# Expert matmuls over 512-column chunks that run across expert borders, in a one-core adaLN block

## The chip, the cores and the metric

The kernel runs on one core of one Trainium2 chip. The metric is the device time of one execution in microseconds. Of the kernel before there are three timed runs and one profiled execution.

## The reference

One block on 4096 tokens of 256 channels, everything in fp32. A state-space mixer (layer norm, projection to 768, a causal convolution, a 16-state scan over the tokens, gating, projection back) is followed by a mixture of 16 experts around one attention. Only the latter's projections are touched:

```python
w = jax.nn.softmax(masked, axis=-1)                # n x 16 expert weights

def moe_proj(p):                                   # p: 16 x 256 x 128
    y = jnp.einsum('nc,ech->neh', x, p)
    return jnp.einsum('ne,neh->nh', w, y)
q = moe_proj(q_proj).reshape(b, t, -1)
k = moe_proj(k_proj).reshape(b, t, -1)
v = moe_proj(v_proj).reshape(b, t, -1)
```

Each token's q, k and v are sums over all 16 experts of the expert's projection times the token's weight for it. Then come softmax attention and an output projection, again summed over experts.

## The kernel before

The tokens are cut into NB = 8 blocks of BT = 512, and each block into TT = 4 tiles of P = 128. The kernel has three parts: preparation of the first block, eight slots with the expert projections (one per block), and attention with the output projection.

A slot has STEPS = 64 steps, one for each tile t and expert e (s = 16 t + e). At a step TensorE multiplies the tile's 128 tokens (256 channels, KC = 2 halves) with the expert's q, k and v weights side by side, H3 = 384 columns (L1470 to L1478). For precision each fp32 operand is split into a high and a low part, and three products are summed: six matmuls per step, all into one PSUM bank. Four banks (MOE_BANKS) are used in turn, and TensorE waits on `moe_acc` until the accumulate of four steps ago is done. VectorE then adds the bank's 384 columns, times the token's weight, onto `acc`: one instruction per step (L1244 for the first expert of a tile, L1247 otherwise), each waiting for `moe_mm` and for the accumulate before it.

`acc` is a part of the tensor `wst`; the high and low weights lie in `w_hi` and `w_lo`, with the layout [P, KC, E, 3, H], so that the experts of one half of the channels are contiguous.

Between the steps both engines run pieces of the work on the following blocks, at step numbers that are written out by hand. Names and steps (later by three in the first slot):
- The scan of the next block has nine links: at steps 1, 3, 5 ... 17 TensorE issues a few small matmuls (`scan_piece`, L1356, L1357, L1359) and VectorE adds their result (`scan_step`, L969). Each link waits for the add before it.
- VectorE's norm pieces of the block after next stand at steps 2, 6, 9, 12 and 15: statistics (L892, L897), modulation (L908), shift (L915), statistics again, normalisation (L902). If a step has both, the norm piece stands before the scan add.
- At step 24 TensorE computes y (L1369), at 27 the output projection of the mixer (L1379), and VectorE adds the residual at 29 (`x2_piece` 0, L996). From step 31 on, six projections (`project`, L1323) follow at one per step; the first waits for that addition. VectorE has convolution pieces (L949) at steps 35 and 39.
- The transposes of the second norm's result stand at step 40 (L1389), the router's logits (L1397) at 44, the input of the scan (L1334) at 49, and VectorE's routing pieces (L1027 to L1090) at 46 to 56.
- At e = 4 of a tile TensorE transposes q and k of the tile before (L1404, L1405), and at e = 6 VectorE takes their low parts (L1119).

Slots 0 to 5 have all of this. Slot 6 has no norms, convolutions or projections, since there is no block after next. Slot 7 has only score maxima for the attention (`max_piece`).

Of the kernel before, what the change touches and what calls it, by code (L numbers as in the profile page):

```python
# [7 lines left out]
ALU = mybir.AluOpType  # L8
# [4 lines left out]
def adaln_block_kernel(nc, x, ln_w, ln_b, w_in, conv_w, a_mat, a_mat_t, bm_t, cm_t, w_out,  # L13
# [84 lines left out]
    with ExitStack() as whole:  # L98
# [234 lines left out]

        STEPS = TT * E
        MOE_BANKS, QK_BANK = 4, 7
        X0, X1, X2 = 4, 5, 6
# [51 lines left out]
        with nc.Block() as block:  # L388
            @block.sync
            def _(sp):  # L390
# [86 lines left out]
                def slot(i, p, ahead):  # L477
# [12 lines left out]
                    if ahead == 0:  # L490
# [4 lines left out]
                        sp.wait_ge(w_ready, NB)  # L495
                        sp.wait_ge(moe_mm, (NB - 1) * STEPS)
                        sp.wait_ge(u_ready, NB)
# [174 lines left out]
            def _(act):  # L672
# [20 lines left out]
                def hidden(i, p):  # L693

                    act.wait_ge(n2_transposed, upto(i, p, 1, 1))

                    wait(act, moe_mm, upto(i, p, STEPS, -2 * STEPS))
                    for k in range(KC):
                        nc.scalar.activation(ht[:, k], ps[:, X1 + k, :], ACT.Identity,
                                             bias=lnb[:, k:k + 1], scale=lnw[:, k:k + 1])  # L700
                        ins = nc.scalar.activation(xt_hi[1 - p][:, k], ps[:, X1 + k, :], ACT.Identity,
                                                   bias=lnb[:, k:k + 1], scale=lnw[:, k:k + 1])
                    ins.then_inc(ht_ready, 1)
# [54 lines left out]
                def x_parts(i, p):  # L758
# [5 lines left out]

                    wait(act, moe_mm, upto(i, p, STEPS, -STEPS))
                    if not (isinstance(i, int) and 2 * i + p == NB - 1):
# [92 lines left out]
                def slot(i, p, ahead):  # L859
# [3 lines left out]
                    else:  # L863
                        act.wait_ge(moe_mm, (NB - 1) * STEPS)
                        act.wait_ge(x2_out, 16 * NB)
# [12 lines left out]
            def _(dve):  # L878
# [354 lines left out]
                def slot(i, p, ahead):  # L1233
                    c, a = following(i, p), (i + 1, p)
                    dve.wait_ge(w_ready, upto(i, p, 1, 1))
                    for s in range(STEPS):
                        t, e = divmod(s, E)

                        dve.wait_ge(moe_mm, upto(i, p, STEPS, s + 1))
                        src, w, dst = ps[:, s % MOE_BANKS, 0:H3], w_cur[:, p, t, e:e + 1], acc[:, t % 2]  # L1240
                        if e == 0:
                            wait(dve, qk_mm, upto(i, p, TT, t - 1))
                            wait(dve, v_split, upto(i, p, TT, t - 1))
                            ts(dst, src, w, None, ALU.mult).then_inc(moe_acc, 1)  # L1244
                        else:
                            dve.wait_ge(moe_acc, upto(i, p, STEPS, s))
                            nc.vector.scalar_tensor_tensor(out=dst, in0=src, scalar=w, in1=dst,  # L1247
                                                           op0=ALU.mult, op1=ALU.add).then_inc(moe_acc, 1)
                        if s == LOW_AT and not (isinstance(i, int) and 2 * i + p == 0):
# [28 lines left out]
            def _(pe):  # L1278
# [186 lines left out]
                def slot(i, p, ahead):  # L1465
                    c, a = following(i, p), (i + 1, p)
                    pe.wait_ge(xlo_ready, upto(i, p, 1, 1))
                    for s in range(STEPS):
                        t, e = divmod(s, E)
                        wait(pe, moe_acc, upto(i, p, STEPS, s - MOE_BANKS + 1))  # L1470
                        rows = slice(t * P, (t + 1) * P)
                        for k in range(KC):
                            for n, (x_part, w_part) in enumerate(((xt_hi, w_hi), (xt_hi, w_lo), (xt_lo, w_hi))):
                                ins = nc.tensor.matmul(  # L1474
                                    ps[:, s % MOE_BANKS, 0:H3], x_part[p][:, k, rows],
                                    w_part[:, k, e].rearrange("p t h -> p (t h)"),
                                    start=(k == 0 and n == 0), stop=(k == KC - 1 and n == 2))
                        ins.then_inc(moe_mm, 1)  # L1478
                        if s == 4 and not (isinstance(i, int) and 2 * i + p == 0):
# [631 lines left out]
```

## Time and profile before

| | us |
|---|---|
| median of 3 runs | 1452.16 |
| lowest, highest run | 1449.67, 1452.58 |
| profiled execution | 1451.81 |
| its span, first to last instruction | 1450.1 |

Engines: PE is TensorE's matmul, PEld its weight load, DVE VectorE, ACT ScalarE, POOL GpSimd, SP SyncE; with a q behind it, the engine's sequencer. The page gives busy time as a share of the span, then 40 equal slices of 36 us each whose digits are the busy share in tenths; PEclk is the granted clock of TensorE in tenths of full speed. A group row reads: line, engine, operation, names out<-in, shapes, count, then busy us and mean ns of one, then the engine's idle time before them and who ended it. A timeline row gives start and duration in us; equal neighbours are merged (x2, x4), with the duration of the merged stretch, and idle time before it stands in brackets.

### The profile page before, as it was taken

What the parts mean: (1) busy time and instruction counts of PE and PEld (TensorE: products, weight loads), DVE (VectorE), ACT (ScalarE), POOL (GpSimd) and SP (SyncE); (2) the same over time, 40 slices, a digit from 0 to 9 for tenths busy, and PEclk for the clock granted to TensorE, in tenths of its full rate; (3) what the DMA queues carried; (4) which work ended last, traced back from release to release, by engine and by line L of the source; (5) the groups of instructions that cost most, each with busy time, mean ns of one, the idle gap of its engine ahead of it and who ended that gap; (6) DMA issues with size and microseconds to landing.
All of it is one profiled execution on the core that took longest, in us unless ns stands there. A gap on an engine that the chain in (4) does not pass through costs nothing. (4 is left out here: it accounts for less than half of the span.)

```text
span 1450.1 us, 20840 instructions
## 1 busy us (share of the span) xinstructions
PE 1375.9 (95%) x6884; PEld 1208.9 (83%) x6884; DVE 1157.6 (80%) x2192; ACT 672.9 (46%) x1331; POOL 709.5 (49%) x628
## 2 busy tenths in 40 slices
PE   5578999999999999999999999999999999999998
PEld 3458989999999999999999966878787887878776
DVE  5758587686875868767677888999999999989876
ACT  3340221302213013131011089888888888888983
POOL 3222131311312213112014167888888888989897
PEclk8688999999999999999999999999999999999999
DMA  4230110011110111010116450010000000000000
GB/s 135 74 97 16 31 39 27 26 39 31 39 27 26 39 31 39 17 37 18 59 46 201 138 194 15 8 37 9 24 21 15 30 16 29 15 28 11 15 16 30
DMA packets 84668, 63.24 MB, mean 44 GB/s; under 512 B 15520, under 2 KB 77392, under 8 KB 84304
## 3 DMA queue, kind: packets, MB, share of 16 engines
q1 hardware_dynamic: 56656, 46.69, 10.3%
q10 hardware_dynamic: 27904, 15.21, 3.6%
q8 instruction: 54, 0.88, 0.3%
q14 instruction: 54, 0.44, 0.1%
HBM read 36.72 MB, written 25.17 MB: 43 GB/s over the span
## 5 line engine op out<-in xcount | busy, mean ns | idle before, releaser
L1474 PE MATMUL ps<-w_hi,memory_r 128*128 128x384 f32 x2048 | 569.2, 343 | 5.7 <-DVE w_lo L887 2.7
L1247 DVE SCALAR_TENSOR_TENSOR wst<-ps,w_cur,wst 128x384 f32<-128x384 f32 x480 | 295.3, 615 | 169.7 <-PE ps L1474 156.3
L1474 PEld LDWEIGHTS ps<-w_hi,memory_r 128*128 128x128 f32 x2048 | 376.2, 189 | 9.9 <-DVE w_lo L887 2.9
L1691 POOL TENSOR_TENSOR memory_rest<-memory_rest,pf 128x512 f32<-128x512 f32 x248 | 346.3, 1396 | 66.9 <-ACT pf L1798 58.3
L1474 PE MATMUL ps<-w_lo,memory_r 128*128 128x384 f32 x1024 | 344.6, 337 | 0.0
L1864 DVE TENSOR_TENSOR p_lo<-pf,p_hi 128x512 fp32r<-128x512 f32 x256 | 282.4, 1103 | 34.2 <-ACT p_hi L1800 33.2
L1474 PEld LDWEIGHTS ps<-w_lo,memory_r 128*128 128x128 f32 x1024 | 194.0, 189 | 4.7 <-issue 1.4
L1798 ACT ACTIVATE pf<-ps 128x512 f32<-128x512 f32 x256 | 153.1, 598 | 71.5 <-PE ps L1970 55.7
L1758 ACT COPY ps<-shift_rows 128x512 f32<-128x512 f32 x254 | 151.7, 597 | 5.9
L1800 ACT ACTIVATE p_hi<-ps 128x512 fp32r<-128x512 f32 x256 | 152.1, 594 | 0.0
L1845 DVE TENSOR_REDUCE mx<-ps 128x1 f32<-128x512 f32 x224 | 147.6, 678 | 1.2 <-PE ps L1959 1.2
L624 POOL TENSOR_TENSOR wst<-wst 128x128 fp32r<-128x128 f32 x28 | 12.9, 462 | 271.5 <-ACT wst L781 271.5
L1881 DVE SCALAR_TENSOR_TENSOR memory_rest<-ps,w_out_s,memory_rest 128x256 f32<-128x256 f32 x252 | 120.7, 479 | 8.2 <-PE ps L2037 3.2
L1671 POOL TENSOR_TENSOR memory_rest<-memory_rest,act_half 128x256 f32<-128x256 f32 x112 | 108.1, 966 | 6.2 <-ACT act_half L1773 1.3
L1994 PE MATMUL ps<-p_hi,memory_kv 128*128 128x512 f32 x256 | 101.0, 395 | 7.4 <-DVE p_lo L1864 7.4
L1968 PE MATMUL ps<-memory_r 128*128 128x512 f32 x256 | 101.8, 398 | 5.8 <-ACT ps L1758 4.5
L2037 PE MATMUL ps<-o_hi,ot_hi 128*128 128x512 f32 x256 | 100.1, 391 | 1.4 <-DVE ot_lo L1886 1.4
L1970 PE MATMUL ps<-memory_r,memory_kv 128*128 128x512 f32 x256 | 100.1, 391 | 0.0
L1969 PE MATMUL ps<-memory_kv,memory_r 128*128 128x512 f32 x256 | 100.1, 391 | 0.0
L1996 PE MATMUL ps<-p_lo,memory_kv 128*128 128x512 f32 x256 | 100.0, 390 | 0.0
L1995 PE MATMUL ps<-p_hi,v_lo 128*128 128x512 f32 x256 | 99.9, 390 | 0.0
L2037 PE MATMUL ps<-o_lo,ot_hi 128*128 128x512 f32 x256 | 99.8, 390 | 0.0
(216 smaller groups left out, 2103.7 us busy)
## 6 DMA issues: line engine op xcount, KB each, us to landing
qk_scratch<-wst ACTq DMA_DIRECT2D x56, 128.0 KB, 2.2
memory<-in_x SPq DMA_DIRECT2D x8, 512.0 KB, 4.1
x_scratch<-memory SPq DMA_DIRECT2D x8, 512.0 KB, 2.9
o_scratch<-memory_rest SPq DMA_DIRECT2D x16, 256.0 KB, 3.2
x2b<-x_scratch SPq DMA_DIRECT2D x32, 128.0 KB, 2.2
out_x<-memory_rest SPq DMA_DIRECT2D x32, 128.0 KB, 1.7
v_scratch<-wst ACTq DMA_DIRECT2D x60, 64.0 KB, 1.8
memory_r<-qk_scratch SPq DMA_DIRECT2D x9, 256.0 KB, 4.5
```

Source lines behind the costliest of these rows:

```text
L1247: nc.vector.scalar_tensor_tensor(out=dst, in0=src, scalar=w, in1=dst, op0=ALU.mult, op1=ALU.add).then_inc(moe_acc, 1)
L1474: ins = nc.tensor.matmul(ps[:, s % MOE_BANKS, 0:H3], x_part[p][:, k, rows], w_part[:, k, e].rearrange("p t h -> p (t h)"), start=(k == 0 a ...
L1671: nc.gpsimd.tensor_tensor(total, total, halves[n], ALU.add).then_inc(act_summed, 1)
L1691: nc.gpsimd.tensor_tensor(p_sum[:, p], p_sum[:, p], pf[:, j % PB], ALU.add).then_inc(p_summed, 1)
L1758: nc.scalar.copy(ps[:, S_BANK + j % 2, :], shift_rows[:]).then_inc(seeded, 1)
L1798: nc.scalar.activation(pf[:, buf], ps[:, S_BANK + j % 2, :], ACT.Exp, scale=SCALE).then_inc(pf_ready, 1)
L1800: nc.scalar.activation(p_hi[:, buf], ps[:, S_BANK + j % 2, :], ACT.Exp, scale=SCALE).then_inc(p_hi_ready, 1)
L1845: nc.vector.tensor_reduce(mx[:, t, g:g + 1], ps[:, MAX_BANKS[j % 2], :], AX_X, ALU.max).then_inc(max_red, 1)
L1864: nc.vector.tensor_tensor(p_lo[:, j % PB], pf[:, j % PB], p_hi[:, j % PB].bitcast(F32), ALU.subtract).then_inc(p_lo_ready, 1)
L1881: nc.vector.scalar_tensor_tensor(out=y[:, t % 2], in0=src, scalar=w, in1=so_far, op0=ALU.mult, op1=ALU.add).then_inc(y_acc, 1)
L1968: nc.tensor.matmul(dst, k_hi[:, keys], q_hi[:, p], start=shifted, stop=False, skip_group_check=True)
L2037: ins = nc.tensor.matmul(dst, a[:, p, rows], b[:, 2 * pair:2 * pair + 2].rearrange("p e c -> p (e c)"), start=(n == 0), stop=(n == 2))
```

## The change

A slot's expert matmuls no longer stop at an expert's 384 columns. The 16 x 384 = 6144 columns of a tile are cut into CHUNKS = 12 chunks of 512, each of which fills a PSUM bank, and a chunk runs across the border between experts. The number of columns is the same; there are 12 groups of six matmuls per tile in place of 16. At step e TensorE issues the chunks that expert e needs and that are not yet issued: one at most steps, none at e = 3, 7, 11, 15. `moe_mm` counts chunks, `moe_acc` still counts experts. The wait for a free bank is now for all experts that read the chunk of four chunks ago.

VectorE sums each expert's 384 columns with one instruction across two neighbouring banks where need be. Where the columns wrap from bank 3 to bank 0 (experts 5 and 10) it takes two, one for each side.

```diff
+        CHUNKS = E * H3 // BT
+        def chunks_for(x):
+            return -(-x * H3 // BT)
+        def readers_of(c):
+            return -(-(c + 1) * BT // H3)
...
-                        dve.wait_ge(moe_mm, upto(i, p, STEPS, s + 1))
-                        src, w, dst = ps[:, s % MOE_BANKS, 0:H3], w_cur[:, p, t, e:e + 1], acc[:, t % 2]
+                        w, dst = w_cur[:, p, t, e:e + 1], acc[:, t % 2]
                         if e == 0:
                             wait(dve, qk_mm, upto(i, p, TT, t - 1))
                             wait(dve, v_split, upto(i, p, TT, t - 1))
-                            ts(dst, src, w, None, ALU.mult).then_inc(moe_acc, 1)
                         else:
                             dve.wait_ge(moe_acc, upto(i, p, STEPS, s))
-                            nc.vector.scalar_tensor_tensor(out=dst, in0=src, scalar=w, in1=dst,
-                                                           op0=ALU.mult, op1=ALU.add).then_inc(moe_acc, 1)
+                        first, last = e * H3 // BT, chunks_for(e + 1) - 1
+                        turn = last * BT - e * H3 if last % MOE_BANKS < first % MOE_BANKS else H3
+                        for c0, c1, chunk in ((0, turn, last if turn == H3 else first), (turn, H3, last)):
+                            if c0 < c1:
+                                bank, at = divmod((e * H3 + c0) % (MOE_BANKS * BT), BT)
+                                src = ps[:, bank:MOE_BANKS, :].rearrange("p b n -> p (b n)")[:, at:at + c1 - c0]
+                                dve.wait_ge(moe_mm, upto(i, p, TT * CHUNKS, t * CHUNKS + chunk + 1))
+                                if e == 0:
+                                    ins = ts(dst[:, c0:c1], src, w, None, ALU.mult)
+                                else:
+                                    ins = nc.vector.scalar_tensor_tensor(out=dst[:, c0:c1], in0=src, scalar=w,
+                                                                         in1=dst[:, c0:c1], op0=ALU.mult, op1=ALU.add)
+                        ins.then_inc(moe_acc, 1)
...
-                        wait(pe, moe_acc, upto(i, p, STEPS, s - MOE_BANKS + 1))
                         rows = slice(t * P, (t + 1) * P)
-                        for k in range(KC):
-                            for n, (x_part, w_part) in enumerate(((xt_hi, w_hi), (xt_hi, w_lo), (xt_lo, w_hi))):
-                                ins = nc.tensor.matmul(
-                                    ps[:, s % MOE_BANKS, 0:H3], x_part[p][:, k, rows],
-                                    w_part[:, k, e].rearrange("p t h -> p (t h)"),
-                                    start=(k == 0 and n == 0), stop=(k == KC - 1 and n == 2))
-                        ins.then_inc(moe_mm, 1)
+                        for chunk in range(chunks_for(e), chunks_for(e + 1)):
+                            t0, c0 = divmod(t * CHUNKS + chunk - MOE_BANKS, CHUNKS)
+                            wait(pe, moe_acc, upto(i, p, STEPS, t0 * E + readers_of(c0)))
+                            for k in range(KC):
+                                cols = slice((k * CHUNKS + chunk) * BT, (k * CHUNKS + chunk + 1) * BT)
+                                for n, (x_part, w_part) in enumerate(((xt_hi, w_hi), (xt_hi, w_lo), (xt_lo, w_hi))):
+                                    ins = nc.tensor.matmul(
+                                        ps[:, chunk % MOE_BANKS, :], x_part[p][:, k, rows],
+                                        w_part[:].rearrange("p k e t h -> p (k e t h)")[:, cols],
+                                        start=(k == 0 and n == 0), stop=(k == KC - 1 and n == 2))
+                            ins.then_inc(moe_mm, 1)
```

The waits of the other engines on `moe_mm` change their counts alone, from STEPS to TT * CHUNKS per slot.

## Rows read from the trace of the kernel before

**Rows 1.** The page: TensorE's busy share, and its granted clock in 40 slices.
```profile
PE 1375.9 (95%) x6884; PEld 1208.9 (83%) x6884; DVE 1157.6 (80%) x2192; ACT 672.9 (46%) x1331; POOL 709.5 (49%) x628
...
PEclk8688999999999999999999999999999999999999
```

**Rows 2.** Windows of slots 2, 5: length; busy PE, PEld, DVE, ACT, POOL; clock; DMA.
```profile
305.80:398.60 92.80, 92.45 (x528) 87.61 (x528) 68.32 (x159) 18.68 (x37) 19.92 (x17) 1.00 0.11 32
...
584.00:676.70 92.70, 92.35 (x527) 87.50 (x526) 68.30 (x158) 18.68 (x37) 19.93 (x17) 1.00 0.09 26
```

**Rows 3.** Groups by line: VectorE's accumulates.
```profile
L1247 DVE SCALAR_TENSOR_TENSOR wst<-ps,w_cur,wst 128x384 f32<-128x384 f32 x480 | 295.3, 615 | 169.7 <-PE ps L1474 156.3
```

**Rows 4.** Timeline of TensorE in slot 4: two scan links and what follows.
```profile
504.04 0.32 PE L1356 MATMUL ps<-scan_a,powers 128*128 128x48 f32 x2
...
504.41 0.42 PE L1474 MATMUL ps<-w_hi,memory_r 128*128 128x384 f32 x1
...
506.94 0.41 PE L1356 MATMUL ps<-scan_b,powers 128*128 128x32 f32 x2 [0.20 <-DVE scan_b L969]
```

**Rows 5.** Timeline of TensorE in slot 3, 21 expert matmuls apart.
```profile
439.93 0.34 PE L1474 MATMUL ps<-w_lo,memory_r 128*128 128x384 f32 x1
...
443.57 0.33 PE L1474 MATMUL ps<-w_lo,memory_r 128*128 128x384 f32 x1
```

**Rows 6.** Timeline of TensorE in the attention, 20 matmuls apart.
```profile
1000.20 0.39 PE L1968 MATMUL ps<-memory_r 128*128 128x512 f32 x1
...
1004.74 0.39 PE L1968 MATMUL ps<-memory_r 128*128 128x512 f32 x1
```

**Rows 7.** Groups by line: VectorE's read of two PSUM banks.
```profile
L996 DVE TENSOR_TENSOR memory<-memory,ps 128x1024 f32<-128x1024 f32 x8 | 9.7, 1213 | 0.5 <-PE ps L1379 0.5
```

**Rows 8.** Timeline of VectorE in slot 4, steps 6 to 13.
```profile
501.21 0.41 DVE L1119 TENSOR_TENSOR wst<-ps,wst 128x256 fp32r<-128x256 f32 x1
501.54 1.66 DVE L908 SCALAR_TENSOR_TENSOR memory<-memory,mv,modv 128x256 f32<-128x256 f32 x4
503.12 0.61 DVE L1247 SCALAR_TENSOR_TENSOR wst<-ps,w_cur,wst 128x384 f32<-128x384 f32 x1
...
503.84 1.34 DVE L1247 SCALAR_TENSOR_TENSOR wst<-ps,w_cur,wst 128x384 f32<-128x384 f32 x2
505.09 1.66 DVE L915 SCALAR_TENSOR_TENSOR memory<-memory,rs,modv 128x256 f32<-128x256 f32 x4
506.68 0.21 DVE L969 TENSOR_TENSOR scan_b<-scan_a,ps 128x64 f32<-128x64 f32 x1
...
509.27 1.40 DVE L892 BATCH_NORM_STATS2 bst<-memory 128x6 f32<-128x256 f32 x4
...
511.11 0.58 DVE L1247 SCALAR_TENSOR_TENSOR wst<-ps,w_cur,wst 128x384 f32<-128x384 f32 x1
```

**Rows 9.** Waits of TensorE in slot 4 (us in total, times, longest).
```profile
PE ps L1359 <- DVE scan_a L969: 0.2, 1, 0.2
```

**Rows 10.** Timeline of slot 4, steps 29 to 31: VectorE, then TensorE.
```profile
534.62 0.62 DVE L1247 SCALAR_TENSOR_TENSOR wst<-ps,w_cur,wst 128x384 f32<-128x384 f32 x1 [0.42 <-PE ps L1474]
535.15 1.21 DVE L996 TENSOR_TENSOR memory<-memory,ps 128x1024 f32<-128x1024 f32 x1
...
536.50 1.59 PE L1323 MATMUL ps<-memory_r 128*128 128x512 f32 x6
```

**Rows 11.** Timeline of slot 4 before the logits: ScalarE's cast, TensorE's first matmul.
```profile
558.11 1.02 ACT L768 CAST memory_r<-ps 128x1024 fp32r<-128x1024 f32 x1
...
559.58 1.07 PE L1397 MATMUL ps<-sn,memory 128*128 128x16 f32 x9
```

**Rows 12.** Timeline of TensorE at slot 0's start and at slot 7's end.
```profile
120.28 0.44 PE L1474 MATMUL ps<-w_hi,memory_r 128*128 128x384 f32 x1 [2.03 <-DVE wst L1244]
...
832.47 0.33 PE L1404 MATMUL ps<-ident,wst 128*128 128x128 f32 x1 [0.71 <-DVE wst L1247]
```

**Rows 13.** Windows, behind slot 7 (columns as in rows 2).
```profile
832.50:840.20 7.70, 4.64 (x15) 2.89 (x15) 2.99 (x6) 3.00 (x8) 1.06 (x2) 0.78 0.49 143
```

More of the change, by code:

```diff
@@ L495, in slot @@
                         sp.wait_ge(w_ready, NB)
-                        sp.wait_ge(moe_mm, (NB - 1) * STEPS)
+                        sp.wait_ge(moe_mm, (NB - 1) * TT * CHUNKS)
                         sp.wait_ge(u_ready, NB)
@@ L695, in hidden @@
                     act.wait_ge(n2_transposed, upto(i, p, 1, 1))
-                    wait(act, moe_mm, upto(i, p, STEPS, -2 * STEPS))
+                    wait(act, moe_mm, upto(i, p, TT * CHUNKS, -2 * TT * CHUNKS))
                     for k in range(KC):
@@ L763, in x_parts @@
                     nc.scalar.copy(h2t, src)
-                    wait(act, moe_mm, upto(i, p, STEPS, -STEPS))
+                    wait(act, moe_mm, upto(i, p, TT * CHUNKS, -TT * CHUNKS))
                     if not (isinstance(i, int) and 2 * i + p == NB - 1):
@@ L863, in slot @@
                     else:
-                        act.wait_ge(moe_mm, (NB - 1) * STEPS)
+                        act.wait_ge(moe_mm, (NB - 1) * TT * CHUNKS)
                         act.wait_ge(x2_out, 16 * NB)
```

## The prediction

> **What bounds the kernel now.** I read the page's busy shares first, then the groups by line, then the timeline of one slot, engine by engine. TensorE is busy 95% of the span and its clock digits are at full from the fourth slice on [rows 1]. The part that changes is the expert stretch, 111.7 to 831.8 us, half of the span: eight slots of 512 tokens. A middle slot takes 92.8 us with TensorE busy for 92.45 of them, while VectorE is busy for 68.3 [rows 2]. So the stretch is paid in TensorE's queue, and VectorE sits idle 169.7 us in front of its accumulates [rows 3]. But VectorE is only just early enough: one link of the scan already holds TensorE for 0.20 us [rows 4]. A gain must show as fewer microseconds in TensorE's queue, and a loss as TensorE waiting for VectorE.
>
> **The matmuls.** Their durations (0.34 us) overlap and say nothing of the rate; starts do. Between 439.93 and 443.57 lie 21 matmuls of 384 columns: 3.64 / 21 = 173.3 ns [rows 5]. In the attention stretch 20 matmuls of 512 columns lie between 1000.20 and 1004.74: 4.54 / 20 = 227 ns [rows 6]. I use 226.7, which puts the difference of the two at 2.4 columns per ns (128 in 53.4 ns) and leaves 13.3 ns per matmul that don't depend on its width. Per tile of 128 tokens: before 96 x 173.3 = 16.64 us, after 72 x 226.7 = 16.32 us. That is 0.32 us per tile, 1.28 per slot of four, 10.2 us for all 32 tiles. 768 weight loads go too, but they lie under the matmuls. Those rates already contain the load, so nothing more is counted.
>
> On this the Trainium skill ("TensorE: Matmul & The Clock Gate", section "Wait — 56ns, not 53.3ns?") gives the width over 2.4 GHz plus about 2.5 ns for back-to-back matmuls. With that rate a tile would go from 15.60 to 15.54 us, 2 us for the kernel instead of 10. These rows show 13.3 ns, and I go by them.
>
> **The accumulates.** Reading across two banks: one VectorE instruction already reads 1024 columns across two banks in 1213 ns, the price of its width and some 150 ns [rows 7], so I take zero for the border (a discount isn't excluded, but I see no row for one). Experts 5 and 10 of each tile wrap from bank 3 to bank 0 and are summed in two pieces: 64 more instructions. Bounds: by duration a 256-column one takes 0.47 us (four of them 1.66, three starts of 1.59 / 4 taken off [rows 8]) against 0.615 for 384 [rows 3], 1.1 ns a column, so two pieces cost 0.21 us more. By start-to-start (pieces of 256 columns start 0.40 us apart, 505.09 to 506.68 for four, and 128 columns take 0.14 less) 0.26 + 0.40 = 0.66 against the 0.53 of an undivided one: 0.13 more. I take 0.13 in the queue. 64 of them are 8 to 13 us of VectorE, of which it has 24 us idle in each slot.
>
> **The banks.** Chunk c+4 must wait for all readers of chunk c. From the end of the last chunk that such a reader needs there are two chunks (2.72 us) or three; before there were three steps (3.12 us). I followed one slot through: the readers are done at least 0.4 us early everywhere, the tightest at step 53 of the routing. So the banks don't bind.
>
> **What is moved.** This is the term that decides. Steps 3, 7, 11 and 15 of each tile now have no chunk of their own, and the pieces that hang on steps (scan links on odd steps, projections, transposes) follow at once on the piece of the step before. Two scan links that lay two steps apart (2 x 1.04 us) now lie one chunk (1.36) apart where an empty step is between, and two chunks elsewhere. VectorE's pieces keep their step, but its accumulate starts only when the chunk is complete. Walk of one middle slot, 0 being its first matmul. Prices: chunk 1.36, plus an estimated 0.09 behind another kind of matmul (the first one behind a link lasts 0.42 against 0.34, rows 4); scan link 0.37 on TensorE (504.04 to 504.41); accumulate to next piece 0.53, accumulate to accumulate 0.72 (505.09 - 503.84 = 1.25 for the two); from the start of VectorE's scan add to TensorE's next link 0.26 (506.68 to 506.94) [rows 4, 8]; from the end of a chunk's issue to its accumulate 0.20 (534.62 against 536.50 less two steps [rows 10]).
> - TensorE ends chunk 5 at 9.99 (six chunks, five switches, three links, carry and two transposes 0.28), chunk 6 at 11.81, chunk 7 at 13.17. VectorE: accumulate 6 at 10.19, low parts 0.33, then the four modulations 1.58 (501.21 to 501.54 to 503.12), accumulate 7 at 12.63, scan add at 13.16: TensorE's link at step 9 waits until 13.42, **0.25**.
> - Accumulates 8, 9 at 13.35 and 14.07, the four shifts 1.59, scan add at 16.19, link released at 16.45. TensorE has only chunk 8 meanwhile (13.79 + 1.45 = 15.24): it waits **1.21**. Before it had steps 10 and 11 there and waited 0.20.
> - Chunks 9, 10: link at step 13 on time (19.68). Statistics 1.84 (509.27 to 511.11), accumulate 13, scan add at 21.39, link released at 21.65. TensorE, with chunk 11 done at 21.26, waits **0.39**. The last link is on time, where it waited 0.2 before [rows 9].
> - Step 31: the first projection needs VectorE's residual sum. That is accumulate 29 to release 0.20 + 0.53 + 1.21 + 0.05 = 1.99 us behind chunk 10's end; TensorE has chunk 11 (1.36): **0.63**. Before, it had two steps, 2.08 us, and went on without idle time [rows 10].
> - Logits at step 44: the high part (ScalarE's cast at 558.11, 1.02 long) was done 0.4 us ahead of the first matmul at 559.58 [rows 11]. Now three chunks lie behind the transposes, but VectorE's low parts are 0.7 us later against the transposes: about **0.2**.
>
> Sum 2.68, less the 0.4 of before: 2.3 us more idle per middle slot, against 1.28 saved: +1.0 each, five slots, **+5.1**. Slot 6 has no norms and no projections in its way: -1.28 + 0.2 = **-1.1**. Slot 7 **-1.3**. In slot 0 all pieces stand three steps later, so that the shifts meet two chunks and only the links at steps 8 and 20 wait (0.3 and 0.7). At its start TensorE waits 2.03 us for the first accumulate [rows 12], and four wider banks carry it 1.3 steps further though it then needs the second accumulate: 0.7 back. Together -1.28 + 1.0 - 0.7 = **-1.0**. At the end of slot 7 the last chunk releases two accumulates where one step released one, and TensorE's transpose waits for the last [rows 12]: **+0.7**. Total 5.1 - 1.1 - 1.3 - 1.0 + 0.7 = +2.4 us, say 2.5. The profiled execution took 1451.81, 0.35 below the median of the runs, which is nothing; **1454.3 us**.
>
> **The rivals.**
> 1. The waits don't come, or half of them do: TensorE's queue shortens by 10 us and VectorE's spare time takes the rest. For it: VectorE is idle a quarter of the slot. Against it: that idle time lies elsewhere, in steps 20 to 34 and at the end, and the link at step 11 already waits. None of them: 1451.8 - 10.2 + 0.7 = 1442; half: about 1448. Chance 0.22.
> 2. The waits are larger than walked: each 0.1 us by which VectorE is later in steps 5 to 15 goes through undiminished, since links alternate between the two. The link at step 5 is on time by only 0.10, and accumulates 5 and 10, now in two pieces, lie in that chain. With 1 us more per middle slot: 1459. Chance 0.12.
> 3. Slower, by the clock: around 832.5 to 840.2, where TensorE was idle 3 of 7.7 us, the granted clock was 0.78 on the mean [rows 13], one fall to the 1.2 GHz level. Now TensorE idles 1.85 us within about 9 us of the scan. If that were enough, such a fall (0.22 x 7.7 us of full rate) costs 1.7 us of work; one in six slots each is +10: 1464.5. It decides from the point where such a stretch first shows below 1.00; before, no middle slot does [rows 2]. Chance 0.10.
> 4. The change doesn't do what it says: inside a group of six that sums into one bank, wide matmuls may run slower than in the attention stretch. The nearest row is the projections' group of six, 1.59 long [rows 10]: less the last one's 0.39, five starts take 1.20, or 240 ns each with the switch in them, so a chunk costs between 1.36 and 1.44, and from 1.387 on nothing is saved: 1454.3 + 10.2 = 1464.5. Chance 0.04. By the page of the skill that is named above the saving would be 2 us.
>
> **How the numbers follow.** The walk holds within 4 us, 1450 to 1458, with 0.52. Range: 1444 to 1462, from a third of the way between rival 1's two ends up to rival 2 and the near edge of the clock's. Something near 0.2% (3 us) can just be told from no change. Of the walk's 0.52 some 0.32 lie within 1449.3 to 1455.1, 0.18 above and 0.02 below. Same: 0.32 and 0.02 from the edge of rival 1, 0.34. Faster: 0.20 of rival 1 and 0.02, 0.22. Slower: 0.18 and rivals 2 to 4, 0.44. The walk's own range, 1450 to 1458, stands beside the wide one because both signs hold weight.
>
> **What would show it.** 2304 matmuls of 512 columns at 227 ns starts; accumulates over two banks at about 615 ns; 64 more accumulate instructions. Idle time of TensorE before the scan links (near 1.2 us at step 11, 0.4 at step 15, 0.25 at step 9) and before the first projection (0.6), released by VectorE. Middle slots of 93.5 to 94, slot 6 of 79, slot 7 of 74.5. The prediction is wrong if middle slots are below 92.5 (no waits), if the clock falls below 1.00 between 215 and 675 us, or if a chunk takes longer than 1.36.

## The result, and the profile after

| | before | after |
|---|---|---|
| median, us | 1452.5 (12 runs) | 1457.28 (12 runs) |
| lowest, highest | 1449.67, 1453.86 | 1455.22, 1459.45 |
| profiled execution, its span | 1451.81, 1450.1 | 1457.76, 1456.0 |

The ratio of after to before is 1.0032, with a 95% interval of 1.0024 to 1.0039. So the kernel became slower, by 4.8 us between the medians, with a quarter fewer matmuls in the expert stretch. The page of after, its busy times, the clock digits and the two groups of the changed lines:

```profile
PE 1371.8 (94%) x6116; PEld 1106.3 (76%) x6116; DVE 1156.9 (79%) x2256; ACT 674.0 (46%) x1331; POOL 710.5 (49%) x628
...
PEclk8688999999999999999999999999999999999999
...
L1495 PE MATMUL ps<-w_hi,memory_r 128*128 128x512 f32 x1536 | 522.9, 402 | 2.6 <-DVE w_lo L896 2.6
L1264 DVE SCALAR_TENSOR_TENSOR wst<-ps,w_cur,wst 128x384 f32<-128x384 f32 (+2 forms) x544 | 305.3, 568 | 173.2 <-PE ps L1495 167.2
```

Against [rows 1] there are 768 matmuls fewer (6884 to 6116) and 64 VectorE instructions more (2192 to 2256). TensorE's busy time fell by 4.1 us and the span rose by 5.9, so the loss is idle time. The accumulates (against [rows 3]) are told apart by shape in the groups of 310 to 580 us of after:

```profile
L1264 DVE SCALAR_TENSOR_TENSOR wst<-ps,w_cur,wst 128x384 f32<-128x384 f32 x147 | 90.3, 615 | 62.7 <-PE ps L1495 61.5
L1264 DVE SCALAR_TENSOR_TENSOR wst<-ps,w_cur,wst 128x256 f32<-128x256 f32 x22 | 10.6, 481 | 6.0 <-PE ps L1495 5.7
L1264 DVE SCALAR_TENSOR_TENSOR wst<-ps,w_cur,wst 128x128 f32<-128x128 f32 x23 | 8.0, 346 | 0.3
```

An undivided accumulate lasts 615 ns, as before, though six of the fourteen undivided ones of a tile now read across two banks (by their place in the tile these six last 613 to 617 ns at the mean, the eight inside one bank 609 to 618). A divided one costs 481 + 346 - 615 = 212 ns more by duration, the 0.21 of the prediction.

TensorE's waits in the same stretch of after (three middle slots and the scan of each):

```profile
PE ps L1374 <- DVE scan_b L978: 2.4, 3, 0.8
PE ps L1341 <- issue: 1.8, 3, 0.6
PE ps L1377 <- DVE scan_b L978: 0.8, 3, 0.3
PE ps L1374 <- DVE scan_a L978: 0.5, 3, 0.2
```

Per slot these are 0.79 before the link at step 11, 0.60 before the first projection, 0.28 at step 15 and 0.15 at step 9, where before had 0.36 in all (0.20 in [rows 4], 0.16 in [rows 9]). In slots 2 and 3 the link at step 5 waits too, 0.17 and 0.15, and these two slots take 93.8 us against 93.4 to 93.5 of slots 4 and 5. The place, in the timeline of slot 4 of after, VectorE beside TensorE at steps 9 to 11:

```profile
508.34 0.21 DVE L978 TENSOR_TENSOR scan_a<-scan_b,ps 128x64 f32<-128x64 f32 x1
508.47 1.27 DVE L1264 SCALAR_TENSOR_TENSOR wst<-ps,w_cur,wst 128x384 f32<-128x384 f32 x2
508.61 0.42 PE L1374 MATMUL ps<-scan_a,powers 128*128 128x48 f32 x2 [0.17 <-DVE scan_a L978]
...
509.65 1.67 DVE L924 SCALAR_TENSOR_TENSOR memory<-memory,rs,modv 128x256 f32<-128x256 f32 x4
...
510.31 0.40 PE L1495 MATMUL ps<-w_hi,memory_r 128*128 128x512 f32 x1
...
511.23 0.22 DVE L978 TENSOR_TENSOR scan_b<-scan_a,ps 128x64 f32<-128x64 f32 x1
...
511.50 0.41 PE L1374 MATMUL ps<-scan_b,powers 128*128 128x32 f32 x2 [0.79 <-DVE scan_b L978]
```

TensorE's only chunk between the two links is over at 510.71. VectorE does two accumulates and the four shifts in the same time and adds the scan at 511.23.

Where the span went, slot by slot. A slot is counted from its first expert matmul to the next slot's, in the timelines of both kernels:

| stretch | before | after | difference | walked |
|---|---|---|---|---|
| start of slot 0 | 111.75 | 109.96 | -1.8 | 0 |
| slot 0 | 101.47 | 101.37 | -0.1 | -1.0 |
| slot 1 | 92.57 | 96.11 | +3.5 | +1.0 |
| slots 2 to 5, mean | 92.69 | 93.60 | +0.9 each | +1.0 each |
| slot 6 | 80.13 | 79.69 | -0.4 | -1.1 |
| slot 7 | 75.07 | 73.48 | -1.6 | -1.3 |
| last expert matmul to the end | 618.3 | 621.0 | +2.7 | +0.7 |

The start of slot 0 lies anywhere between 110 and 112 in the traces of this case, whichever the kernel, so it is no part of the change. The middle slots' share is the one that was walked. Windows of slots 4 and 1 of after (against [rows 2]; us, busy PE, PEld, DVE, ACT, POOL, clock, DMA share, GB/s):

```profile
494.97:588.42 93.45, 91.62 (x430) 74.33 (x429) 68.45 (x166) 18.61 (x37) 19.97 (x17) 1.00 0.11 31
```
```profile
211.33:307.44 96.11, 93.50 (x430) 75.53 (x429) 67.09 (x166) 18.72 (x37) 19.96 (x17) 0.98 0.11 30
```

Slot 1 is the exception, 2.65 us longer than slot 4, with the clock at 0.98. Its timeline in after, ScalarE and TensorE before the logits (L1415), and the window behind them. Last, the same second issue in slot 1 of before and in slot 4 of after:

```profile
276.51 0.53 ACTq L798 DMA_DIRECT2D qk_scratch<-wst  x1
...
277.08 1.67 ACTq L798 DMA_DIRECT2D qk_scratch<-wst  x1
...
280.91 1.02 ACT L777 CAST memory_r<-ps 128x1024 fp32r<-128x1024 f32 x1
...
281.98 2.09 PE L1415 MATMUL ps<-sn,memory 128*128 128x16 f32 x16 [0.81 <-ACT memory_r L777]
...
283.91 0.78 PE L1495 MATMUL ps<-w_hi,memory_r 128*128 128x512 f32 x1
```
```profile
283.70:287.10 3.40, 3.40 (x11) 2.72 (x11) 0.17 (x1) 0.91 (x1) 3.40 (x2) 0.50 0.00 0
```
```profile
277.15 0.64 ACTq L789 DMA_DIRECT2D qk_scratch<-wst  x1
```
```profile
560.69 0.64 ACTq L798 DMA_DIRECT2D qk_scratch<-wst  x1
```

ScalarE's second DMA issue takes 1.67 us; the same place takes 0.64 in before and in slot 4 of after. ScalarE's queue holds two more issues, a copy (L772) and the cast of L777 behind it, one after the other. So the cast starts 3.83 us behind the start of that issue, where slot 4 has 2.80. In slot 4 it is done 0.11 us ahead of the logits; here TensorE waits 0.81 for it. From 283.7 on, when the sixteen matmuls of 16 columns behind that wait are nearly through, the granted clock is 0.50, the 1.2 GHz level, for 3.4 us. That costs 0.81 and 1.7 us: nearly all of the 2.65.

### The profile page after: what moved, and what is told of

Its sections match the earlier page's. It is cut to its first block and busy times, and to the rows that moved or that the text cites. A ratio compares the mean times of both kernels' runs of the same rounds, so it can differ in the third digit from the quotient of the medians.

```text
span 1456.0 us, 19368 instructions
## 1 busy us (share of the span) xinstructions
PE 1371.8 (94%) x6116; PEld 1106.3 (76%) x6116; DVE 1156.9 (79%) x2256; ACT 674.0 (46%) x1331; POOL 710.5 (49%) x628
## 5 line engine op out<-in xcount | busy, mean ns | idle before, releaser
L1495 PE MATMUL ps<-w_hi,memory_r 128*128 128x512 f32 x1536 | 522.9, 402 | 2.6 <-DVE w_lo L896 2.6
L1264 DVE SCALAR_TENSOR_TENSOR wst<-ps,w_cur,wst 128x384 f32<-128x384 f32 (+2 forms) x544 | 305.3, 568 | 173.2 <-PE ps L1495 167.2
L1495 PEld LDWEIGHTS ps<-w_hi,memory_r 128*128 128x128 f32 x1536 | 291.2, 190 | 62.7 <-DVE w_lo L896 2.7
L1495 PE MATMUL ps<-w_lo,memory_r 128*128 128x512 f32 x768 | 301.4, 392 | 0.0
L1495 PEld LDWEIGHTS ps<-w_lo,memory_r 128*128 128x128 f32 x768 | 146.1, 190 | 28.2 <-issue 1.4
L2058 PE MATMUL ps<-o_hi,ot_lo 128*128 128x512 f32 x256 | 100.5, 392 | 0.0
```

The source lines that it names most:

```text
L1264: ins = nc.vector.scalar_tensor_tensor(out=dst[:, c0:c1], in0=src, scalar=w, in1=dst[:, c0:c1], op0=ALU.mult, op1=ALU.add)
L1495: ins = nc.tensor.matmul(ps[:, chunk % MOE_BANKS, :], x_part[p][:, k, rows], w_part[:].rearrange("p k e t h -> p (k e t h)")[:, cols], sta ...
L2058: ins = nc.tensor.matmul(dst, a[:, p, rows], b[:, 2 * pair:2 * pair + 2].rearrange("p e c -> p (e c)"), start=(n == 0), stop=(n == 2))
```

## The experiments

Ten runs followed, nine of them of new versions and one of the changed kernel again. They are told in the order of the questions, each beside runs of the kernel before on the same chip.

**1. Is the accumulate in two pieces a cost of its own?** The kernel before, with experts 5 and 10 summed in two pieces:

```diff
+                            parts = {5: ((0, P), (P, H3)), 10: ((0, 2 * P), (2 * P, H3))}.get(e, ((0, H3),))
+                            for c0, c1 in parts:
+                                ins = nc.vector.scalar_tensor_tensor(out=dst[:, c0:c1], in0=src[:, c0:c1], scalar=w,
+                                                                     in1=dst[:, c0:c1], op0=ALU.mult, op1=ALU.add)
+                            ins.then_inc(moe_acc, 1)
```

> The kernel before, with the accumulates of experts 5 and 10 of each tile done in two pieces (128 + 256 and 256 + 128 columns), all else as it was. It measures the disputed price of the 64 additional instructions. Theory: VectorE's queue gets 0.13 us longer at each, of which only those on the scan's chain (steps 5 and 10 of a tile's first quarter) reach TensorE: within 1 us of 1452.5. Rival (two pieces are what makes the changed kernel slow): at least 3 us more.

Measured 1452.42 us, ratio 0.9999 (0.9990 to 1.0008); middle slots 92.6 to 92.8, as before. VectorE took the 64 instructions out of its idle time. TensorE's waits in its middle slots are near those of before (0.20 and 0.14). Alone the two pieces cost nothing that can be measured (the interval leaves room for 1.2 us).

**2. Is the wait at step 11 the norm piece ahead of the scan's sum?** The changed kernel, with `scan_step` ahead of the norm piece of the same step:

```diff
-                            if r in DVE_PIECES:
-                                kind, n = DVE_PIECES[r]
-                                piece(n, kind, c, a, ahead)
                             if r in SCAN_AT:
                                 scan_step(SCAN_AT[r], *c)
...
+                            if r in DVE_PIECES:
+                                kind, n = DVE_PIECES[r]
+                                piece(n, kind, c, a, ahead)
```

> The changed kernel, with one thing moved: where a step has both a norm piece and a scan add on VectorE (steps 9 and 15), the scan add comes first. My theory (the loss is TensorE waiting for scan adds that come late): the wait at step 11, 0.8 us of idle time by the profile and near 0.95 by matmul starts, goes in each middle slot; the statistics piece at step 12 then meets a TensorE that is earlier, so that the wait at step 15 grows from 0.45 to some 0.9. Net 0.5 us per middle slot, 2.5 in all: about 1454.8. Rival (the wider matmul or the cross-bank accumulate itself costs the time, the order of pieces is of no account): 1457.3 as it was.

Measured 1452.65 us, ratio 0.9997 (0.9987 to 1.0006). TensorE's waits in slots 2 to 5:

```profile
PE ps L1341 <- issue: 2.4, 4, 0.6
PE ps L1377 <- DVE scan_b L978: 1.7, 4, 0.4
PE ps L1374 <- DVE scan_a L978: 0.5, 3, 0.2
```

The wait at step 11 is gone. The one at step 15 grew from 0.28 to 0.43, not to the 0.9 that was expected: TensorE comes there 0.8 us earlier, and VectorE not quite as much. Slots 2 to 5 take 92.5 to 92.85, on the level of before. So slots 1 to 5 gave back 4.9 us together, twice the 2.5 that were expected, and slot 0 another 2 (99.41), of which nothing was expected. VectorE has the same work in both kernels. So its order, and not its load, was the cause of this wait. In slot 1 the wait before the logits (0.57) and a fall of the clock (at 283.1) stayed.

**3. Is the wait at step 31 the missing chunk?** The changed kernel, all projections one step later:

```diff
-        PE_TRANSPOSE_N2, PE_Y, PE_OUT, PE_PROJECT, PE_TRANSPOSE_H2, PE_LOGITS, PE_BU = 19, 24, 27, 31, 40, 44, 49
+        PE_TRANSPOSE_N2, PE_Y, PE_OUT, PE_PROJECT, PE_TRANSPOSE_H2, PE_LOGITS, PE_BU = 19, 24, 27, 32, 40, 44, 49
```

> The changed kernel, with the six projections of TensorE one step later (32 to 37), so that a whole chunk lies between chunk 11 and the first of them. Theory: the wait of 0.6 (0.76 by starts) for the residual sum goes in slots 1 to 5, and the later pieces are still on time: 3.8 us less, 1453.5. Rival: the same wait comes back before the transposes of step 40 or the logits of step 44, since the norm behind the residual sum is what is late: 1457.

Measured 1453.29 us, ratio 1.0003 (0.9993 to 1.0012). In the changed kernel the profile names no releaser for this wait ("issue"), but the projection starts as soon as VectorE's residual sum has ended (timeline of its slot 4):

```profile
540.29 1.21 DVE L1005 TENSOR_TENSOR memory<-memory,ps 128x1024 f32<-128x1024 f32 x1
...
541.60 1.60 PE L1341 MATMUL ps<-memory_r 128*128 128x512 f32 x6 [0.60 <-issue]
```

One step later that cover is back. No wait at L1341 is left in the middle slots, which take 92.55 to 92.95. That the time meets the 1453.5 of the expectation owes much to luck, since two things that it did not have partly cancel. In slot 1 all four of ScalarE's issues together took 2.56 us (3.23 in the changed kernel's), the logits waited for nothing, and the slot gave back 3.5 us. But slot 0 took 105.50: TensorE waited 3.6 us for the second norm before its transposes (L1407), where it had waited 2.25, and the clock fell behind that for 6.8 us (at 186.1). In slot 0 the same step numbers, three later, meet other work. (The profiled execution is the slowest of its ten, 1455.72, so a usual slot 0 may be shorter.)

**4. What are the chunks worth without these waits?** Both edits, norm pieces at 3, 7, 11, 15 and 17 (on steps with no chunk of their own, or behind the link), transposes at 20. First in the changed kernel (4 runs), then the very same places in the kernel before:

```diff
-            0: ("carry", 0), 2: ("norm", 0), 6: ("norm", 1), 9: ("norm", 2), 12: ("norm", 3), 15: ("norm", 4),
+            0: ("carry", 0), 3: ("norm", 0), 7: ("norm", 1), 11: ("norm", 2), 15: ("norm", 3), 17: ("norm", 4),
```

> The changed kernel with all pieces placed for the chunks: scan add ahead of the norm piece, norm pieces at steps 3, 7, 11, 15 and 17 (each behind a scan add that has two chunks behind it), transposes of the first norm at 20, projections from 32 on. Theory: all four waits of a middle slot go (2.5 us by starts), 12 us over five slots: 1445, clearly faster than the kernel before. Rival (VectorE as a whole is too slow for the wide chunks, or the matmuls don't save): the waits turn up elsewhere, not below 1452.5.

> The kernel before, with 384-column steps, and the same new places for the pieces as in the retimed changed kernel. Theory: only its two short waits per middle slot go (0.35 us by the profile, 0.7 by starts): 1449 to 1451. The difference to the retimed changed kernel is then the worth of the wide matmuls alone: 10.2 us by the walk, less the later end of slot 7 (1.4) and what the slower starts cost, so 5 to 9. Rival (it was the places, not the chunks, that matter): the two retimed kernels take the same time.

The changed kernel took 1445.63 us, ratio 0.9950 (0.9933 to 0.9966); the kernel before took 1451.76, 0.9991 (0.9982 to 1.0000). Slot 4 of the former, a stretch of 91 us of the latter, and TensorE's waits in slots 2 to 5 of the former, all there are:

```profile
488.43:579.40 90.97, 90.73 (x430) 74.75 (x429) 68.45 (x166) 18.58 (x37) 20.00 (x17) 1.00 0.11 32
```
```profile
490.00:581.00 91.00, 91.00 (x524) 86.93 (x523) 66.98 (x157) 18.59 (x37) 19.75 (x17) 1.00 0.11 32
```
```profile
PE ps L1325 <- DVE memory L911: 1.0, 4, 0.2
```

With the waits gone a middle slot takes 91.0 us in chunks and 91.65 in steps. So the chunks are worth 0.7 us per slot (some 0.9 without the wait of 0.24 left at L1325), and 6.1 us for the kernel, of which 2.4 are slot 0 (103.44 against 105.86, where the clock fell for 3.4 and for 6.8 us). They are that only where VectorE's pieces have places that suit them. The changed kernel gains 11.7 us from the new places (1457.28 to 1445.63), the kernel before only 0.9 (1452.66 to 1451.76, on one chip). That is less than the 1.5 to 3.5 that were expected, but not because its middle slots gained little: slots 1 to 5 together fell by 4.7 us, from 463.3 to 458.6. Its slot 0 lost 4.4 (101.47 to 105.86), with waits of 1.0 and 2.0 us for accumulates and the clock at 0.50 for 6.8 us from 187.3 on. So the new places help both kernels in the middle slots and hurt both in slot 0.

**5. Slot 1: does it come back, and does a later step for the logits cure it?** First the changed kernel once more (a single run), then with the logits at step 45:

```diff
-        PE_TRANSPOSE_N2, PE_Y, PE_OUT, PE_PROJECT, PE_TRANSPOSE_H2, PE_LOGITS, PE_BU = 19, 24, 27, 31, 40, 44, 49
+        PE_TRANSPOSE_N2, PE_Y, PE_OUT, PE_PROJECT, PE_TRANSPOSE_H2, PE_LOGITS, PE_BU = 19, 24, 27, 31, 40, 45, 49
```

> The changed kernel as it is, looked at once more, for the clock: its profile showed one fall to the 1.2 GHz level inside a slot, at 283.7 us in slot 1, right behind a wait of 0.8 us before the logits, whose cause was a DMA issue of ScalarE that took 1.67 us in place of 0.64. Theory (such a fall follows from the wait and the small matmuls of the logits): the fall is again there if the long issue is, in the same slot. Rival (the falls are strewn by chance): another place or none, whatever the issue does.

> The changed kernel with the router's logits one step later (45), so that a late high part finds TensorE at a chunk. Theory: slot 1's wait of 0.8 and the fall of the clock behind it, 2.6 us more than in the slots after it, go; the middle slots stay at 93.5: 1454.5 to 1455.5. Rival (the fall has nothing to do with that wait): 1457, the fall as before.

Once more: 1458.34 us, with the issue at 1.47 us, a wait of 0.61 and the fall at 284.6, in slot 1 again and in no other middle slot. With the later logits: 1455.28 us, ratio 1.0018 (1.0009 to 1.0027). Its timeline:

```profile
278.07 1.86 ACTq L798 DMA_DIRECT2D qk_scratch<-wst  x1
...
283.13 0.40 PE L1495 MATMUL ps<-w_hi,memory_r 128*128 128x512 f32 x1
...
283.37 1.85 PE L1415 MATMUL ps<-sn,memory 128*128 128x16 f32 x16
```

The issue is long again, longer even, but TensorE has a chunk to run and no wait, and the clock stays at full: slot 1 takes 93.37. Of the 4.8 us that the change cost, 2.0 were this one place by the medians, 2.7 by the slot.

The long issue is no chance of one execution. One of the four issues ahead of the cast is long in slot 1 of all nine traces of kernels with chunks: the second in the changed kernel (twice), in that of experiment 2 and in this one, the third in the other five (0.95 to 1.58 us in place of 0.56). At this place none is long in the three traces of kernels with steps, nor in slots 2 to 5 of any trace. The trace's DMA packets show what it coincides with. Queue q8, of the kind "instruction", has only 54 packets in before and 48 in after. Of the 1728 DMA issues of ScalarE in the twelve traces 18 last longer than 0.85 us, these nine among them, and each of the 18 has a q8 packet that starts between 0.55 us ahead of it and 0.15 us into it. In slot 1 of the kernels with steps no such packet falls there. It isn't enough alone: of 30 issues with a packet in that place 18 are long. That the packet causes the delay is not shown, as no run moved it by itself.

**6. The ends.** The re-timed kernel, with slot 0's pieces four steps later in place of three, and the last maximum at step 63:

```diff
-        MAX_STEPS = {8 + 7 * n // 4: n for n in range(TT * KG)}
+        MAX_STEPS = {8 + 7 * n // 4 + (n == TT * KG - 1): n for n in range(TT * KG)}
...
-            return 3 if isinstance(i, int) and 2 * i + p == 0 else 0
+            return 4 if isinstance(i, int) and 2 * i + p == 0 else 0
```

> The retimed changed kernel (all pieces placed for the chunks), and besides the first slot's pieces four steps late in place of three, so that they meet the chunks as in the other slots, and the last score maximum behind both last accumulates. Theory: of slot 0's waits (3.6 us before the transposes of the second norm, 1.0 before those of the first, and a fall of the clock behind them, together some 3 us over the other slots' share) 2 to 3 us go, and 0.5 at the end of slot 7: 1442 to 1443.5. Rival (slot 0's waits come from data that arrive late, not from the grid of steps): 1445 to 1446.

A miss: 1447.19 us, ratio 0.9957 (0.9943 to 0.9971), no better than without (0.9950). TensorE no longer waits for the carry (2.55 in the re-timed kernel), but VectorE is late for accumulates that TensorE's banks need. Slot 0 of this kernel:

```profile
119.76 0.50 PE L1495 MATMUL ps<-w_hi,memory_r 128*128 128x512 f32 x1 [1.78 <-DVE wst L1264]
...
151.58 0.50 PE L1495 MATMUL ps<-w_hi,memory_r 128*128 128x512 f32 x1 [1.37 <-DVE wst L1264]
...
185.10 0.50 PE L1495 MATMUL ps<-w_hi,memory_r 128*128 128x512 f32 x1 [2.32 <-DVE wst L1264]
189.84 0.47 PE L1407 MATMUL ps<-ident,memory 128*128 128x128 f32 x1 [2.14 <-DVE memory L924]
```

The clock fell at 185.5 for 10.2 us, and the slot took 106.73. In slot 1 the third issue took 1.58 us, a wait of only 0.25 before the logits had a fall of 3.4 us behind it (at 287.9), and that slot took 93.0. (The profiled execution is the slowest of its five, 1449.81.) Of the last maximum's move, the wait for the last sum shrank from 1.60 to 1.26 us; the kernel's time doesn't show it.

**7. Slot 0 given its own places.** The re-timed kernel with slot 0 as in experiment 2, and the same with the logits at 45:

```diff
+        FIRST_NORMS = {2: 0, 6: 1, 9: 2, 12: 3, 15: 4}
+        FIRST_PIECES = {r: piece for r, piece in DVE_PIECES.items() if piece[0] != "norm"}
+        FIRST_PIECES.update({r: ("norm", n) for r, n in FIRST_NORMS.items()})
...
+        def pe_places(i, p):
+            return (19, 31) if late(i, p) else (PE_TRANSPOSE_N2, PE_PROJECT)
```

> The re-timed version of the changed kernel, but with the first slot's pieces at the steps at which the changed kernel with the scan's sum first had them (projections from step 31, norm pieces at 2, 6, 9, 12 and 15, all three later). The theory: the re-timed version's first slot took 103.44 us against 99.41 there, because its projections lie one step later; with that the residual's norm came late, TensorE waited 3.6 us for the transposes (L1407) and the granted clock fell behind that. The first slot gives back 3.5 to 4.0 us and the kernel takes 1441.5 to 1442.5 us; no clock fall at 188, the other slots stay at 91.0. The rival, that the first slot's wait comes from the other queues' work at its start (weights, the later norm pieces): the first slot stays above 102 and the kernel takes 1444.5 to 1446.

> The kernel with the first slot's pieces put back, and the router's logits at step 45 in place of 44 in every slot. The theory, that the logits' wait at 0.6 to 0.8 us and the clock fall behind it come only where ScalarE's DMA issue ahead of the cast is a long one: here it changes nothing where that issue is short (1441.5 to 1442.5, the same as without it within 0.5) and saves about 2 us where one is long; there must be no wait of TensorE at L1415 in slots 1 to 5. The rival, that a later step for the logits makes the routing behind it late: TensorE waits at the input of the scan or at the next slot's first link, each slot is 0.2 us or more longer, and the kernel takes 1443.5 or more.

Measured 1443.98 us, ratio 0.9938 (0.9922 to 0.9955), and 1441.35 us, ratio 0.9920 (0.9905 to 0.9935). The last is the fastest version of this case, 11.6 us faster than the kernel before. Not all of that is the chunks': the places alone took 4.7 us off slots 1 to 5 of the kernel before (experiment 4). No run has the kernel before with the new places and slot 0 left as it was; by the slots it would take some 1448 us, an estimate from 1452.5 less 4.7. The first is a miss on slot 0: it took 102.28, above 102 as the rival had it, and not 99.4 (103.44 without the edit). The wait at L1407 fell from 3.6 to 2.24, as in the kernel of experiment 2, but the clock fell behind it here, and the carry waits 3.1 us in place of 2.6. The second kernel's slot 0 is the same, 102.30, and slot 1 has no wait at the logits, though that wasn't needed in the first either. Of the 2.6 us between the two medians the profiled spans show 0.9 (1442.2 and 1441.3; the second is the slowest of its four): 0.4 of it is slot 6, where the wait of 0.12 before the logits is gone, and the first one's trace has a clock fall at 1413.6 that the second's lacks. So the later logits cost nothing and gain 0.4 us in slot 6; that they gain more in the re-timed kernel is not shown.

## Why the prediction was right or wrong

The sign, the size in the middle slots and their reason were right. The forecast of 1454.3 is 3 us below the measured 1457.28, which lies in the upper part of the range. Of the change itself the forecast had 2.1 us (against 1452.16) and the runs show 4.8, so the total was less than half, and the range of 18 us is wide beside both. Of the prediction's own signs of being wrong two came, though the middle slots are as forecast: the clock fell below 1.00 between 215 and 675 us (slot 1), and a chunk takes 1.37 us (6 x 228.3 ns), a hair above 1.36.

**The matmuls.** Mis-sized, by 0.3 us a slot. The starts behind one another are 173 and 227 ns at the median, as in [rows 5, 6], but of 245 such starts in slot 4 of after 57 take 231 to 236 ns (18 of 340 in before take 178 or more). The means are 173.8 and 228.3, so a slot saves 384 x 173.8 - 288 x 228.3 = 1.0 us, not 1.28. The walk took two stretches without such starts and the medians with them. By the rate of the Trainium skill ("TensorE: Matmul & The Clock Gate", section "Wait — 56ns, not 53.3ns?") a slot would have saved an estimated 0.25 us. These starts carry 14 to 15 ns beyond their width at 2.4 GHz (173.8 - 160, 228.3 - 213.3), and the measurement decides.

**The waits.** The walk's places were right: step 9, 11, 15 and the first projection. It had the link at step 5 on time by 0.10, and in slots 2 and 3 that link waits as well. Its sizes were 0.25, 1.21, 0.39 and 0.63, the profile's gaps are 0.15, 0.79, 0.28 and 0.60. But a gap begins at the modelled end of the last matmul, 0.39 after its start, and the next one would have started 0.23 after it; so each wait is 0.16 longer than its gap (before: 0.34 and 0.173, the same 0.16). By starts the four are 0.33, 0.96, 0.45 and 0.76, together 2.5, which is the walk's own 2.48. Step 11 was 0.25 too large and the other three too small by as much together. Its two causes are small. From the release of the link at step 9 to that of the link at step 11 VectorE takes 2.89 us (508.61 to 511.50), where the walk had 3.03, half of it because two accumulates in a row are 0.65 apart (508.47) and not 0.72, a price from one pair of [rows 8]. TensorE takes 1.93 for link and chunk, where the walk had 1.82. What was mis-sized is the sum around the four: 0.2 for the logits that middle slots don't wait for, and 0.4 for before, which was read off gaps and is 0.69 by starts. So the waits grew by 1.8, not 2.3, and the chunks saved 1.0, not 1.28. The two errors cancelled: +0.9 per middle slot measured, +1.0 walked.

**The banks.** Right in slots 1 to 5: TensorE waits for no accumulate there. The border between banks costs nothing (613 to 617 ns against 609 to 618), and the two pieces nothing that can be measured (experiment 1).

**The logits, 0.2.** This step failed. In slots 2 to 5 nothing is waited for: the cast is done 0.11 ahead. In slot 1 the wait is 0.81, and the clock falls. The walk had the margin of 0.4 from one slot [rows 11] and moved VectorE's low parts against it; it didn't ask what ScalarE's queue holds ahead of the cast. Those are DMA issues, whose length varies (0.64 to 1.86 us at this place). In before none is long in slot 1; with its margin of 0.44 an issue longer by 1.03 would have cost some 0.6 us there too, an estimate. Experiment 5 shows the 2 us.

**Rival 3, the clock.** Neither as priced nor absent. The waits at the scan, 1.2 us by gaps and 1.7 by starts where the rival had 1.85, never lowered the clock in the five middle slots of four traces with them. A single wait of 0.6 to 0.8 us ahead of matmuls of 16 columns did, twice in the changed kernel and once in that of experiment 2 (and one of 0.25 in experiment 6), while those of 0.11 to 0.13 in slot 6 never did. The rival had the right price for a fall, 1.7 us, but put it at the scan, and six times.

**Slot 0.** The "0.7 back" was wrong. Four wider banks did carry TensorE past the first accumulate (the 2.03 of [rows 12] is gone), but only to the scan's first link, which waits for the carry:

```profile
120.49 0.69 PE L1374 MATMUL ps<-scan_a,powers 128*128 128x63 f32 x2 [3.12 <-DVE scan_a L970]
```

Before, it waited 2.03 and then 0.90 for the carry: 2.93 against 3.12. The walk removed a wait and didn't say what is late next. The transposes of this slot wait 2.25 too, before 1.94 in two parts.

**Slot 6 and slot 7.** Slot 7 gained 1.6 (walked 1.3; the 74.5 us among the prediction's signs does not fit its own walk, 75.1 less 1.3). Slot 6 gained 0.4 (walked 1.1): new waits of 0.34 for the second norm and 0.11 for the logits' cast stand there, where 0.2 was walked.

**The end of slot 7.** Right in kind, small in size. The transpose now waits 1.60, before 0.71, since the last chunk releases two accumulates, with a maximum between them:

```profile
835.13 0.62 DVE L1264 SCALAR_TENSOR_TENSOR wst<-ps,w_cur,wst 128x384 f32<-128x384 f32 x1 [0.74 <-PE ps L1495]
835.67 0.55 DVE L1135 TENSOR_REDUCE mx<-ps 128x1 f32<-128x384 f32 x1
836.13 0.61 DVE L1264 SCALAR_TENSOR_TENSOR wst<-ps,w_cur,wst 128x384 f32<-128x384 f32 x1
...
836.80 0.33 PE L1422 MATMUL ps<-ident,wst 128*128 128x128 f32 x1 [1.60 <-DVE wst L1264]
```

The attention's first matmul starts 4.58 us after the last expert matmul's end, 1.06 more than before (3.52). Of the rest of the +2.7 some 1.1 are a clock fall at 1427.1 in the attention. Such a fall, between 1413 and 1428, is in four more traces of changed kernels (those of experiments 3 and 5 and the first of 7) and missing in the other four (experiments 2 and 6, the re-timed one, the fastest) and in the three of kernels with steps, so whether it belongs to the change stays open.

Together, the forecast missed by the fall in slot 1 (+2.5), slot 0 and 6 (+1.5) and the end (+2.0), less 1.8 us by which slot 0 began early, less 0.4 in four middle slots together and 0.3 in slot 7: +3.5, as is 1457.76 - 1454.3 of the profiled execution, which lies 0.5 above its median. That the slip of 3 us is no larger is luck in part: the early start of slot 0 is not the change's.

## What to carry to other kernels

When the steps of a hand-timed pipeline change their length, the saving stands in the matmul queue and the bill in the other engines' queues: walk every piece that hung on a step again, and move the pieces with the steps. Here the same chunks cost 5 us with the old places and saved 6 with the same new places in both kernels. And move the pieces in the old version too before crediting the change: its middle slots gained 4.7 us by that alone. Where a small piece follows a dependency with under a microsecond of margin, look at what else its producer's queue holds ahead of it, DMA issues above all, and give it one more piece of long work as cover.

## What the runs showed of the hardware that was not expected

The length of a DMA issue on ScalarE varies at one and the same place of the program: 0.64 us in slot 4 of after, and in slot 1 0.64 in before, 1.67 and 1.47 in two executions of after, 1.42 in experiment 2 and 1.86 with the later logits. Work queued behind it on ScalarE moves by as much. All 18 of ScalarE's issues over 0.85 us in the twelve traces coincide with a packet of the instruction queue q8 (experiment 5). Such a packet comes every 20 to 32 us in the expert stretch of both kernels, and the change, with its 768 matmuls fewer, has moved them: they start at 248.6, 277.2 and 308.1 in slot 1 of after, at 226.6, 248.7, 272.1 and 295.4 in that of before.

The same wait can let the clock fall or not. In slot 0 of the kernel of experiment 2, and in after, TensorE waits 2.25 us for its transposes and runs all eight at full clock; in the last kernel of experiment 7 the wait is as long, the eight take longer, and the clock is at 0.50 for 3.4 us. First after, then the latter and its window:

```profile
185.27 1.09 PE L1407 MATMUL ps<-ident,memory 128*128 128x128 f32 x8 [2.25 <-DVE memory L924]
```
```profile
185.21 1.92 PE L1417 MATMUL ps<-ident,memory 128*128 128x128 f32 x8 [2.25 <-DVE memory L934]
```
```profile
185.30:188.70 3.40, 3.40 (x13) 3.01 (x14) 3.36 (x7) 2.58 (x10) 1.50 (x2) 0.50 0.39 116
```

What tells the two apart is not in these rows, and so the clock's share of a forecast has a spread of a fall or two, at 1.7 us each, that no walk of the queues removes.
